# Graph attention layers: gathering the first five groups of rows at the end of the stage ahead

## The reference

```python
for i in range(NUM_LAYERS):            # 3
    residual = h_cur @ W_res + b_res if i == 0 else h_cur
    h_t = _transformer_conv(h_cur, src_idx, dst_idx, edge_attr, Wq[i], bq[i], Wk[i], ...)
    h_cur = jax.nn.relu(h_t + residual)

# _transformer_conv, with 3 heads of 128 features
ke = k[src] + e                        # rows of the source nodes, one for each edge
alpha = (q[dst] * ke).sum(-1) / jnp.sqrt(C)
ex = jnp.exp(alpha - amax[dst])
w = ex / (den[dst] + 1e-16)
msg = (v[src] + e) * w[:, :, None]
out = jax.ops.segment_sum(msg, dst, num_segments=n)
```

## Time and profile before

| | us |
|---|---|
| three launches | 3851.28, 3863.35, 3868.51 |
| their median | 3863.35 |
| the profiled launch | 3844.19 |
| its span (first to last instruction) | 3842.3 |
| POOL busy, share of the span | 1784.3, 46% |
| PE busy, share of the span | 3290.5, 86% |

### The profile page before, as it was taken

The page is one execution under the profiler, slowest core; times in us unless marked ns, Lnnn a source line. Parts: engine busy times, 40 slices in busy tenths (PEclk is TensorE's granted clock), DMA queues, the critical chain, the costliest instruction groups (busy, mean ns, idle before and its releaser), DMA issues. The chain is left out here.

```text
span 3842.3 us, 81259 instructions
## 1 busy us (share of the span) xinstructions
PE 3290.5 (86%) x22381; PEld 2019.8 (53%) x22381; DVE 1831.5 (48%) x5337; ACT 1453.3 (38%) x3467; POOL 1784.3 (46%) x1807
## 2 busy tenths in 40 slices
PE   3999989974776999996888888688888789999998
PEld 1666666653554565653555554344444445555554
DVE  4676767766653444442444444344444332352222
ACT  3555555541272454542333333133333231131112
POOL 1554555530026777773777777377777500000000
PEclk8999999997898999998999899689999989999999
DMA  4677777656556666664878788477777555442223
GB/s 120 187 213 201 213 200 198 187 146 160 176 148 173 170 184 176 184 176 122 228 215 232 208 219 223 114 210 213 201 207 209 139 178 183 174 143 98 71 106 122
DMA packets 717296, 675.29 MB, mean 176 GB/s; under 512 B 383127, under 2 KB 543713, under 8 KB 716885
## 3 DMA queue, kind: packets, MB, share of 16 engines
q1 hardware_dynamic: 623366, 466.26, 41.6%
q0 software_dynamic: 77008, 200.24, 19.9%
q10 hardware_dynamic: 16768, 6.91, 0.7%
HBM read 530.84 MB, written 142.28 MB: 175 GB/s over the span
## 5 line engine op out<-in xcount | busy, mean ns | idle before, releaser
L2199 POOL DMA_INDIRECT l_y<-s_lrows,l_src x1332 | 1331.4, 1000 | 443.4 <-issue 381.7
L3202 PE MATMUL ps<-nl_adj,nl_table 126*128 126x504 bf16 (+1 forms) x3150 | 631.8, 357 | 2.3 <-DVE nl_table L3437 2.3
L960 POOL DMA_INDIRECT em_gs<-s_rows,em_idx x400 | 392.6, 982 | 352.9 <-DMA em_idx<-in_sd 240.8
L2239 PE MATMUL ps<-ident,l_y 128*128 128x128 f32 x1800 | 270.7, 287 | 226.0 <-DMA l_y<-s_lrows,l_src 142.7
L3202 PEld LDWEIGHTS ps<-nl_adj,nl_table 126*128 126x128 bf16 x3150 | 301.9, 96 | 299.3 <-issue 6.0
L2593 DVE TENSOR_TENSOR l_y<-l_y 128x768 f32<-128x768 f32 x225 | 214.1, 952 | 368.4 <-DMA l_y<-s_lrows,l_src 327.2
L2282 PE MATMUL ps<-l_y,aw_pT 128*63 128x277 f32 x2700 | 375.3, 415 | 2.5 <-ACT aw_pT L2476 1.7
L2462 ACT ACTIVATE aw_yT<-ps 128x512 f32<-128x512 f32 (+1 forms) x525 | 261.6, 534 | 277.6 <-PE ps L2239 268.8
L2239 PEld LDWEIGHTS ps<-ident,l_y 128*128 128x128 f32 x1800 | 206.7, 145 | 285.8 <-issue 221.7
L2266 PE MATMUL ps<-aw_yT,aw_qt 128*63 128x384 f32 x1800 | 335.2, 495 | 6.3 <-DMA aw_yT<-s_dxT 6.3
L2476 ACT ACTIVATE aw_pT<-ps 128x381 f32<-128x381 f32 x225 | 110.1, 489 | 460.4 <-PE ps L2274 446.4
(11 more groups left out here) (375 smaller groups left out, 5759.4 us busy)
## 6 DMA issues: line engine op xcount, KB each, us to landing
nl_adj<-s_adj SPq DMA_DIRECT2D x20, 3100.8 KB
aw_yT<-s_dxT SPq DMA_DIRECT2D x150, 384.0 KB, 4.4
aw_geoS<-s_geoS SPq DMA_DIRECT2D x450, 94.5 KB
nl_adj<-s_adj SPq DMA_DIRECT2D x15, 2325.6 KB
ws_msg<-s_msg SPq DMA_DIRECT2D x75, 384.0 KB, 3.8
s_dxT<-aw_yT SPq DMA_DIRECT2D x75, 384.0 KB, 2.9
aw_qt<-s_qt SPq DMA_DIRECT2D x225, 126.0 KB
s_msg<-em_msg SPq DMA_DIRECT2D x100, 256.0 KB, 2.9
```

The source lines that it names most:

```text
L960: pool.indirect_dma_start(out=gs[:, u, j, :], out_offset=None, in_=d["rows0"], in_offset=bass.IndirectOffsetOnAxis(ap=idx[:, u, 2 * j:2 * ...
L2199: pool.indirect_dma_start(out=y[:, u, j, 0:W], out_offset=None, in_=table, in_offset=bass.IndirectOffsetOnAxis(ap=src[:, u, j:j + 1], axis ...
L2239: m = nc.tensor.transpose(k.ps[:, FEATURES[n], q * 128:(q + 1) * 128], y[:, u, j, what * D:(what + 1) * D], k.ident[:, :])
L3202: m = nc.tensor.matmul(k.ps[:, bank(i, p), 0:cols * WN], source[:, p, q, b, :], adj[:, a % 2, 0:cols, b * WN:(b + 1) * WN], start=b == 0 a ...
```

## The change

`first_index` copies the indices of five windows in place of one. `first_rows` issues the gathers of groups 0 to 4, 30 indirect DMAs in place of 6. The round's own block no longer issues groups 1 to 4 and no longer copies their indices. The loop over groups 5 to 74 is as it was. There are still 450 gathers in a round, with the same sizes.

```diff
+FIRST_GROUPS = 5
...
-    k.nc.vector.tensor_copy(k.src[:, 0, :].unsqueeze(1), k.sd[:, 0:1, :].rearrange("p w (t s) -> p w t s", s=2)[:, :, :, 0]
+    k.nc.vector.tensor_copy(k.src[:, 0:FIRST_GROUPS, :], k.sd[:, 0:FIRST_GROUPS, :].rearrange("p w (t s) -> p w t s", s=2)[:, :, :, 0]
                             ).then_inc(indexed, 1)
...
-    for j in range(T):
-        pool.indirect_dma_start(out=k.y[:, 0, j, 0:D if l == 0 else 2 * D], out_offset=None, in_=k.dram[f"lrows{l}"],
-                                in_offset=bass.IndirectOffsetOnAxis(ap=k.src[:, 0, j:j + 1], axis=0)).then_inc(k.rows_in[0], 16)
+    for u in range(FIRST_GROUPS):
+        for j in range(T):
+            pool.indirect_dma_start(out=k.y[:, u, j, 0:D if l == 0 else 2 * D], out_offset=None, in_=k.dram[f"lrows{l}"],
+                                    in_offset=bass.IndirectOffsetOnAxis(ap=k.src[:, u, j:j + 1], axis=0)).then_inc(k.rows_in[u], 16)
...
-            for u in range(1, U):
-                gather(u, u)
             with pool.Fori(1, NW // U) as i:
...
-            dve.sem_inc(indexed.sem, 1)
-            for u in range(1, U):
-                indices(u, u)
+            dve.sem_inc(indexed.sem, FIRST_GROUPS)
             weigh(0, 0, 0)
```

## The result

| | before | changed |
|---|---|---|
| median | 3862.51 us (3851.28 to 3868.51, 4 launches) | 3943.95 us (3935.44 to 3962.8, 4 launches) |
| span of the profiled launch | 3842.3 us | 3960.7 us |

The ratio is 1.0221, with a 95% interval of 1.0173 to 1.0269. That is +85 us on 3862.5, with an interval of +67 to +104 us. The changed kernel is slower.

The account below looks back on a forecast made before the run. POOL's gathers were taken to bound each round, at some 7.7 us a window. Group 6's delays of 31.8, 30.1 and 28.1 us, together 90.0, less 5 gave +85 us: median 3948 us, 2.2% slower, range 3915 to 3975 us.

Parts of the forecast that it names:

- POOL is the pace and the ends of the blocks wait for it: Inside rounds POOL sets some 7.7 us a window; at three block ends it arrives last, by 0.2, 6.0 and 4.6 us.
- The releases move by 31.8, 31.2 and 31.5 us: Block ends before rounds 0, 1 and 2: the 24 moved gathers delay the next block by their full length.
- rival A: Round start: start-up gives back the full 13.9 us and moved gathers run faster; +72 us, median 3935 us, chance 0.18.
- The drain's tail stays: Block ends: POOL's drain after its last gather keeps its length, +0; upper bound together +16.8 us.
- Rival B: Block ends: POOL's drain grows with gathers queued ahead, up to 11.3 us each; +102 us, median 3965 us, chance 0.14.
- Group 5 needs slot 0, and group 6 follows the sums of window 1: Round start: POOL waits for slots, idle 35 to 45 us; group 6 later by 31.8, 30.1 and 28.1 us.
- The start-up gives back 5 us: Round start: first loads and weights no longer compete with the 24 gathers; 5 us taken, bounds 0 and 13.9 us.
- Sum: Three rounds together: 90.0 us later at group 6, less 5 us from the start-up, +85 us.
- Rival C: Block's end doesn't wait for POOL's gathers: about -9 us, median 3854 us, chance 0.04.
- Rival D: Inside rounds PE and DVE, not POOL, are the pace and later groups catch up: time stays at 3863 us, chance 0.04.

Follow-up runs that it names:

- twice: Kernel before, with the 24 gathers of groups 1 to 4 added at the end of the stage ahead and repeated in the round: 1.0197, +76 us.
- drop: Kernel before, with 20 of the 24 gathers of groups 1 to 4 left out in each round: 0.9972, -11 us.
- r0: Five groups gathered ahead in round 0 alone, one in rounds 1 and 2, against the kernel before: 1.0072, +28 us.
- r12: Five groups gathered ahead in rounds 1 and 2 alone, one in round 0, against the kernel before: 1.0145, +56 us.

## Why the prediction was right

The forecast was a median of 3948 us, and it was 3943.95. Each step against what was measured:

- *POOL is the pace and the ends of the blocks wait for it.* Right. POOL's drain ends 31 to 35 us behind SP's, and `twice` shows that nothing hides it.
- *The releases move by 31.8, 31.2 and 31.5 us.* They moved by 30.4, 30.5 and 29.9 us against the round's first gather (40.3, 45.2 and 44.8 us in place of 9.9, 14.6 and 14.9). The moved gathers have none of 1.6 us or more among them, and take 1.25 us each with the gap. This part of rival A was right, the term was 3.7 us too large in all.
- *The drain's tail stays.* 2.8, 7.4 and 7.4 us, where it had been 2.3, 7.4 and 7.4. Rival B falls.
- *Group 5 needs slot 0, and group 6 follows the sums of window 1.* Right, with the idle times of 39.7, 35.7 and 32.4 us. I had forecast 35 to 45 us, so round 2 fell 2.6 us short.
- *The start-up gives back 5 us.* The sums of window 1 ended 45.2, 39.1 and 39.0 us after the release, where they had ended 47.7, 40.2 and 38.1. That is 2.7 us in all. The load waits did shrink: PE's wait for the weights in round 0 from 5.4 to 3.2 us, for the queries from 6.9 to 5.2 us in round 1 and from 5.5 to 4.9 us in round 2. But in round 2 the third window's transfer stands behind SP's loads, and PE's wait for it grew from 6.3 to 8.9 us. The term was too large by 2.3 us, for the reason that I had written beside it.
- *Sum:* releases +90.8, start-up -2.7, slack of POOL behind the slots in rounds 1 and 2 -4.5, together +83.6 us, by the trace. That I came within 1.4 us of it is partly luck: my two errors, +3.7 and -2.3, nearly cancelled. The first time alone, +67 to +104 us, would have fitted rival A (+72) and rival B (+102) as well. The traces decide between them.
- *Rival C* (the block's end doesn't wait) is ruled out by `twice`, and its bound by the slots was about right: `drop` gives 11 us, where I had about 9.
- *Rival D* (later groups catch up) is ruled out: in no kernel with more groups ahead is the time clearly below the loss at group 6.

The Trainium skill ("DMA: Bandwidth & Descriptors", "Queues, rings and completion order") says that a DMA engine takes turns between its queues, a packet at a time. If the loads had got back every turn, the sum would have been 76 us. Of the 13.9 us that this allowed, 2.7 us reached the path, so the rule can't be read as a price here. No run shows the turns themselves.

Two things stay open. Why TensorE's clock fell more often in rounds 1 and 2 of the one profiled launch of the changed kernel, and why gathers took longer there, isn't known. And the cause of the length of the drain's tail was not found.

## What to carry to other kernels

Work that is moved ahead of a point where all engines meet is hidden only if its engine would be idle there and not the last to arrive. Look first who arrives last, and by how much. Prefetching as many groups as there are slots also means that the next one must wait for the first to be consumed; in the new stage, leave the engine that sets the pace enough work to cover the start-up of the others. Where a start-up is bare, ask for its next wait before shortening one: here 8 us taken from TensorE's mixing turned into 8 us of waiting for a transfer queued behind other loads.

## What the hardware showed

POOL's DRAIN goes on after the last indirect gather has ended, by 1.9 to 7.4 us at these boundaries, and not by a fixed amount. At the ends of rounds 0 and 1 it was 7.4 us behind 6, 12, 18 or 30 gathers alike, but 5.5 us at the end of round 0 in `r0` and in `drop`, 4.0 us in `twice` and 2.9 us behind 30 gathers of the same rows in `r12`. At the end of "mid", with rows of half the size, it was 1.9 to 2.9 us. So neither the number of gathers nor the length of their rows sets it alone. The gathers themselves kept to a median of 0.94 to 0.95 us and a gap of 0.30 us.
